# A cross-attention stage on one core: query copies laid once, stacks by one masked product, three PSUM banks in rotation

## What is computed

```python
q = _split_heads(query @ wq.T + bq, B)      # query: layernorm(x), 16 heads of depth 8
k = _split_heads(value @ wk.T + bk, B)      # value: context, 1500 rows
v = _split_heads(value @ wv.T + bv, B)
scores = jnp.einsum('bhqd,bhkd->bhqk', q, k) / scale
attn = jax.nn.softmax(scores, axis=-1)
ctx = jnp.einsum('bhqk,bhkd->bhqd', attn, v)
return ctx.transpose(0, 2, 1, 3).reshape(B, -1, D_MODEL) @ wo.T + bo
```

## Time and profile before

| | us |
|---|---|
| median of 3 runs | 771.29 (770.04 to 772.39) |
| the profiled execution | 769.12 |
| its span, first to last instruction | 767.3 |

### The profile page before, as it was taken

One profiled execution on the slowest core, in us unless ns is written; L12 is line 12 of the kernel. 1 busy time (PEld: TensorE's weight loads), 2 busy tenths in 40 slices (PEclk: granted clock), 3 DMA queues, 4 the chain that ended last, 5 costly groups with the idle time before them and its releaser, 6 DMA issues. The chain is left out here.

```text
span 767.3 us, 17218 instructions
## 1 busy us (share of the span) xinstructions
PE 665.7 (87%) x6570; PEld 520.1 (68%) x6570; DVE 465.4 (61%) x856; ACT 356.0 (46%) x533; POOL 200.1 (26%) x130
## 2 busy tenths in 40 slices
PE   1689968668999999999999999999999849999998
PEld 0334436435777777777777777777778738999997
DVE  4689737486665665675666666666577146443443
ACT  0335534413556556546555656555644625333321
POOL 2687323253123213213303312321300022111110
PEclk9999958867999999999999999999999958999999
DMA  5000000282165355435426426525526001111200
GB/s 192 0 1 1 1 0 1 49 175 61 51 153 122 86 116 120 104 96 124 120 77 155 109 61 155 120 63 137 121 50 156 3 9 43 43 41 43 80 14 25
DMA packets 16298, 59.04 MB, mean 77 GB/s; under 512 B 4488, under 2 KB 5384, under 8 KB 16264
## 3 DMA queue, kind: packets, MB, share of 16 engines
q1 hardware_dynamic: 16264, 58.57, 31.3%
HBM read 20.73 MB, written 0.46 MB: 28 GB/s over the span
## 5 line engine op out<-in xcount | busy, mean ns | idle before, releaser
L996 DVE TENSOR_REDUCE chunk_max<-PS 128x1 f32<-128x500 f32 x336 | 220.1, 671 | 114.2 <-PE PS L1093 113.6
L949 ACT ACTIVATE P<-PS 125x896 f32<-125x896 f32 x192 | 174.9, 918 | 137.5 <-PE PS L1123 132.2
L1093 PE MATMUL PS<-k_hi,q_block_hi 128*128 128x500 f32 x336 | 155.8, 483 | 11.8 <-DVE chunk_max L996 5.1
L1123 PE MATMUL PS<-q_stack,k_stack 97*125 97x224 f32 x768 | 123.0, 283 | 1.0 <-ACT P L949 0.8
L1123 PEld LDWEIGHTS PS<-q_stack,k_stack 97*125 97x125 f32 x768 | 108.4, 189 | 19.6 <-issue 10.9
L1093 PEld LDWEIGHTS PS<-k_hi,q_block_hi 128*128 128x128 f32 x336 | 65.5, 196 | 41.1 <-DVE chunk_max L996 24.5
L239 POOL TENSOR_TENSOR k_lo<-k_full,k_hi 128x500 fp32r<-128x500 f32 x48 | 60.1, 1254 | 102.4 <-ACT k_full L229 102.4
L1139 PE MATMUL PS<-P,values 125*32 125x112 f32 x3072 | 83.6, 260 | 0.0
L1139 PEld LDWEIGHTS PS<-P,values 125*32 125x32 f32 x3072 | 72.0, 110 | 15.0 <-issue 7.3
L1438 DVE TENSOR_TENSOR hidden<-gated,PS 128x448 f32<-128x448 f32 x64 | 39.5, 619 | 69.0 <-PE PS L1495 64.3
L913 POOL TENSOR_TENSOR q_block_hi<-q_hi,consts 128x896 fp32r<-128x896 f32 x16 | 27.4, 1715 | 192.7 <-PE PS L1109 188.4
(11 more groups left out here) (145 smaller groups left out, 824.9 us busy)
## 6 DMA issues: line engine op xcount, KB each, us to landing
k_stack<-k_hi SPq DMA_DIRECT2D x128, 187.5 KB, 4.7
ctxT<-ctx_in SPq DMA_DIRECT2D x16, 750.0 KB, 4.3
k_stack<-k_lo SPq DMA_DIRECT2D x64, 187.5 KB, 4.5
w_gate_up<-wgu_in SPq DMA_DIRECT2D x8, 512.0 KB, 4.0
w_down<-wd_in SPq DMA_DIRECT2D x8, 256.0 KB, 2.8
mats<-mats_in SPq DMA_DIRECT2D x1, 832.0 KB, 6.3
X<-x_in SPq DMA_DIRECT2D x1, 512.0 KB, 3.6
consts<-consts_in SPq DMA_DIRECT2D x1, 490.0 KB, 4.2
```

Of the source, the lines that this page charges most:

```text
L949: nc.scalar.activation(P[:, t % RING, :].rearrange("p (a n) -> p a n", a=2), PS[0:KR, 2 * (t % 2):2 * (t % 2) + 2, 0:HALF], ACT.Exp).then_ ...
L996: nc.vector.tensor_reduce(out=chunk_max[:, n // KC, n % KC:n % KC + 1], in_=PS[:, max_bank(b, j, n), 0:KW], axis=AX.X, op=ALU.max).then_in ...
L1093: nc.tensor.matmul(PS[:, max_bank(b, j, n), 0:KW], q_block_hi[:, j, 128 * t:128 * t + 128], k_hi[:, j, KW * c:KW * c + KW], start=True, st ...
L1123: last = nc.tensor.matmul(PS[0:KR, 2 * (t % 2) + g // 2, o:o + GH * N], k_stack[:, j, g, KR * t:KR * t + KR], q_stack[0:SHIFT_ROW + 1, j, ...
```

## The change

- **Query copies.** Before period 0 SyncE lays high, high and low parts of all queries, of each group of four heads, in `q_copies` on 96 partitions (`load_copies`, twelve DMAs, runs of 56 elements). `q_lo` as a tensor, `q_block_lo`, the selection matrices `sel` and `max_col` go.
- **Stack by one product.** GpSimd makes rows 0 to 95 of the whole stack by one multiplication of the batch's copies by the head mask (`stack_queries`).
- **Maxima by a transpose.** VectorE joins the maxima into `max_turn`, TensorE transposes them (`turn_max`, slots 3 and 8), ScalarE negates the 4 and 3 rows into `neg_rows`, and SyncE carries each row of 128 elements to row 96 of the stack by a DMA of its own (`load_shift`, 4 + 3 DMAs). Scores of slot 0 wait for them.
- **Three banks.** Chunks of the maximum, keys, values, output and turned maxima take banks 4, 5 and 7 in rotation (`bank_turns`: 30 uses in a period), each behind a wait for the reader of the use three before. The denominators move to the free half of bank 6, and the first weighing of a batch now waits for the reciprocals.
- **Keys.** ScalarE still reads each projection twice; the first read has a semaphore of its own, `k_hi_ready`, on which the chunks wait. Its waits for the free buffers stand behind the wait for the projection.
- **Order.** New `MAX_PLACES` (8 chunks ahead instead of 2) and new slots for all kinds. SyncE issues the stack first, then four rows, then the context, now of batch b+3, then three rows.

```diff
-            EARLY = 10
-            MAX_PLACES = [(1, 1, 0), (1, 1, 1), (1, 0, 0), (1, 1, 0), (1, 0, 0), (1, 1, 1),
-                          (1, 0, 0), (1, 1, 0), (1, 1, 0), (1, 1, 0), (0, 1, 0), (1, 0, 0)]
-            KEY_SLOTS, VALUE_SLOTS, STACK_SLOTS, DEN_SLOT, OUT_SLOT = [0, 1, 3], [2, 4, 5], [8, 10], 6, 11
-            RING, QUAD, WEIGH_SLOTS = 6, 4, [1, 5, 9]
+            EARLY = 8
+            MAX_PLACES = [(2, 0, 2), (0, 0, 0), (1, 2, 0), (1, 0, 0), (0, 1, 0), (1, 0, 1),
+                          (1, 0, 0), (1, 0, 0), (1, 0, 0), (2, 1, 1), (0, 0, 1), (0, 1, 1)]
+            KEY_SLOTS, VALUE_SLOTS, TURN_SLOTS = [2, 3, 4], [1, 6, 7], [3, 8]
+            SUMS_SLOT, DEN_SLOT, INVERT_SLOTS, SCALE_SLOT, OUT_SLOT = 1, 2, [3, 4], 4, 8
+            RING, QUAD, WEIGH_SLOTS = 6, 4, [0, 5, 9]
+            TURNING_BANKS = [4, 5, 7]
...
+            def bank_turns():
+
+                bank_of, uses = {}, 0
+                for t in range(KT):
+                    first, second, third = max_chunks(t)
+                    before = [("max", n) for n in first]
+                    for name, slots in (("key", KEY_SLOTS), ("value", VALUE_SLOTS), ("out", [OUT_SLOT]), ("turn", TURN_SLOTS)):
+                        if t in slots:
+                            before.append((name, slots.index(t)))
+                    for use in before + [("max", n) for n in (*second, *third)]:
+                        bank_of[use] = TURNING_BANKS[uses % len(TURNING_BANKS)]
+                        uses += 1
...
+                    def load_shift(b, j, a):
+
+                        sp.wait_ge(rows_ready, 2 * b + a + 1)
+                        for r, t in enumerate(range(HALF_TILES[a].start, HALF_TILES[a].stop)):
+                            sp.dma_start(q_stack[SHIFT_ROW:SHIFT_ROW + 1, j, 128 * t:128 * t + 128].bitcast(F32),
+                                         neg_rows[r:r + 1, j, a, :].bitcast(F32)).then_inc(shift_loaded[j], 16)
...
+                    load_copies()
+                    sp.wait_ge(v_projected, KC)
+                    load_ctx(sp, 2, 0)
+                    for a in range(2):
+                        load_shift(0, 0, a)
 
                     def period(b, j, u):
-                        if exists(b + 2, B):
-                            sp.wait_ge(cleared, 1)
-                            sp.wait_ge(v_projected, KC * (b + 1))
-                            load_ctx(sp, b + 2, j)
                         if exists(b + 1, B):
                             load_stack(b + 1, 1 - j)
+                            load_shift(b + 1, 1 - j, 0)
+                        if exists(b + 3, B):
+                            sp.wait_ge(v_projected, KC * (b + 2))
+                            load_ctx(sp, b + 3, 1 - j)
+                        if exists(b + 1, B):
+                            load_shift(b + 1, 1 - j, 1)
...
+                    def stack_queries(b, j):
+
+                        lay = [SHIFT_ROW, GROUPS, GH, N]
+                        own = C["quarter"][0:SHIFT_ROW, :].unsqueeze(1).unsqueeze(3).broadcast_to(lay)
+                        nc.gpsimd.tensor_tensor(
+                            q_stack[0:SHIFT_ROW, j, :].rearrange("p (g h n) -> p g h n", g=GROUPS, h=GH),
+                            q_copies[:, :, bass.ds(b, 1), :].bitcast(F32).broadcast_to(lay), own, ALU.mult
+                            ).then_inc(q_stacked, 1)
...
-                    def select_queries(b, j, a):
-
-                        pe.wait_ge(q_blocks, 2 * b + 2)
+                    def turn_max(b, a):
+
                         pe.wait_ge(max_ready, 2 * b + a + 1)
-                        shared_bank((q_stacked, 2 * b + a + 1))
...
+                        if later(b, 1):
+                            take_bank(BANK_OF["turn", a], (rows_ready, 2 * b + a + 1))
+                        elif a == 1:
+                            pe.wait_ge(rows_ready, 1)
+                        nc.tensor.transpose(turn_bank(b, a)[:, 0:128], max_turn[:, a, :], C["ident"]).then_inc(max_turned, 1)
 
                     def scores(b, j, u, t):
 
                         if t == 0:
                             pe.wait_ge(stack_loaded[j], 16 * STACK_DMAS * (u + 1))
-                            pe.wait_ge(q_stacked, 2 * (b + 1))
+                            pe.wait_ge(q_stacked, b + 1)
+                            pe.wait_ge(shift_loaded[j], 16 * QT7 * (u + 1))
```

More of the change, by code:

```diff
@@ L216, in first_keys, with read_keys @@
                 project_keys(pe, b, b, 0, c)
[L218 to L223, removed]
+        def read_keys(act, b, j, u, c, bank=MISC):
             if later(b, 1):
@@ L227, in read_keys, with split_keys @@
             k = slice(KW * c, KW * c + KW)
[L228 to L232, removed]
+            if c == 0 and later(b, 2):
+                act.wait_ge(stack_loaded[j], 16 * STACK_DMAS * u)
+                act.wait_ge(max_scored, QT7 * KC * (b - 1))
+            nc.scalar.activation(k_hi[:, j, k], bank[:, 0:KW], ACT.Identity, bias=COL["bk"]).then_inc(k_hi_ready, 1)
+            nc.scalar.activation(k_full[:, k], bank[:, 0:KW], ACT.Identity, bias=COL["bk"]).then_inc(k_ready, 1)
+        def split_keys(pool, b, j, u):
             if later(b, 2):
@@ L824, in max_batch, with bank, max_bank, turn_bank @@
                 return (b + 2, j) if t >= EARLY else (b + 1, 1 - j)
-            STACK_DMAS = 3 * GROUPS
+            def bank_turns():
[9 more added lines that the diff above has]
+                        uses += 1
+                assert uses % len(TURNING_BANKS) == 0
+                return bank_of
+            BANK_OF = bank_turns()
+            def bank(name, n):
+                return PS[:, BANK_OF[name, n], :]
+            def max_bank(b, n):
+                return BANK_OF["max", n] if later(b, 1) else (n + 4) % 6
+            def turn_bank(b, a):
+                return bank("turn", a) if later(b, 1) else MISC
             q_all = sb2("q_all", [128, B * PITCH])
@@ L865, in build @@
             OSUM = PS[:, 6, 0:4 * N]
+            DEN = PS[:, 6, 4 * N:8 * N]
+            OUT2 = bank("out", 0)[:, 0:D]
             with nc.Block() as block:
@@ L1017, in invert @@
                         dve.wait_ge(den_done, b + 1)
-                        nc.vector.reciprocal(heads_out2[:, half], MISC[:, half]).then_inc(den_inverted, 1)
+                        nc.vector.reciprocal(heads_out2[:, half], DEN[:, half]).then_inc(den_inverted, 1)
                     def scale_heads(b):
@@ L1147, in denominators @@
                         pe.wait_ge(o_copied, b + 1)
[L1148 to L1149 removed]
+                        nc.tensor.matmul(DEN, C["den"], heads_sum[:, :], start=True, stop=True
                                          ).then_inc(den_done, 1)
```

174 lines of the change are left out of this document (89 added, 85 removed).

## The result

The changed kernel takes 714.79 us (median of four runs, 713.22 to 717.7), beside 770.66 us for the kernel before on the same chip: a ratio of 0.929 [0.924, 0.934]. The forecast was 708.0 us with a range of 698 to 730, so the median is 6.8 us above it and inside the range. The profiled execution took 713.22 us, span 711.4; before it was 769.12 and 767.3.

A forecast was written before the change was run, and what follows sets the result against it. TensorE was taken to bound the kernel. Gains of -1.4 (start), 4.1 (first period), 55.5 (thirteen steady periods) and 5.1 (last but one) sum to 63.3 us, taking the median 771.29 to 708.0; range 698 to 730.

The forecast's parts named there:

- Work per period: TensorE, steady period: 24.21 us of work, less 1.82 for the selections, plus 0.54 for two transposes, gives 22.93.
- both turnings: TensorE, two transposes of the maxima per period: 0.27 us each, 0.54 together, from eight like them taking 2.16.
- a changed pitch of the weighings: Sign of a wrong prediction: TensorE's start-to-start time for a block of weighings differs from 1.97 us.
- Waits of the rotation: Three banks: slot 3's chunk waits about 0.6 us for the keys' bank, slot 0's scores 0.1; period 23.6.
- Thirteen periods: Steady periods 1 to 13 of the cross attention: each falls from 27.87 to 23.6 us, 55.5 gained.
- Row DMAs: Last three shift rows before slot 0's scores: a 5.1 us chain just hidden by 5.1 us of TensorE work.
- Rival A: Scores of slot 0: late row DMAs set the period, 24.4 us (time 718) to 25.8 (736); chance 0.27.
- Period 14: Last period but one, 13 chunks and no keys: 18.65 us plus 0.7, so 19.4, a gain of 5.1.
- Rival B: TensorE's waits only move to other places, ScalarE's key reads above all; only the selection gains, 751 us; chance 0.06.
- Rival C: Slower than before: shift rows wait behind larger transfers at slot 0; break-even 4.9 us a period; chance 0.04.
- Before period 0: Start of batch 0's scores, after query copies, GpSimd's product and row DMAs: net 1.4 us later.
- Period 0 and period 15: First period 21.7 us, a gain of 4.1, with 1.5 for the low clock; last period unchanged, gain 0.

The follow-up runs named there:

- The kernel without the key wait: Changed kernel, but ScalarE reads each key projection from PSUM once and makes the rounded copy from SBUF: 707.92 us.
- the rows cut in two: Changed kernel with each row of shifts carried by two DMAs of 64 elements instead of one of 128: 726.97 us.
- The kernel with 3.6 us of it: Changed kernel with the old chunk places (two ahead instead of eight), maxima turned at slots 8 and 10: 817.98 us.
- the filled kernel: Changed kernel with chunks two ahead, plus 15 short unused matmuls ahead of the scores of slot 0: 782.61 us.

## Why the prediction was right, and where it was off

**Work per period (22.93): the sum fits, two of its terms do not.** The kernel without the key wait has a period of 22.90 to 22.97. Luck has a part in that. The changed kernel in order of time:

```profile
291.61 1.00 PE L196 MATMUL PS<-ctxT,mats 128*128 128x500 f32 x2
...
292.99 1.01 PE L196 MATMUL PS<-ctxT,mats 128*128 128x500 f32 x2
...
294.71 0.39 PE L1155 MATMUL PS<-k_hi,q_block_hi 128*128 128x500 f32 x1
295.03 1.74 PE L1195 MATMUL PS<-P,values 125*32 125x112 f32 x64
296.70 0.49 PE L1155 MATMUL PS<-k_hi,q_block_hi 128*128 128x500 f32 x1
297.03 0.60 PE L1179 MATMUL PS<-q_stack,k_stack 97*125 97x224 f32 x4
```

From 291.61 to 292.99 stand a key projection, a turning and the scores of a slot: 1.38 us, less 0.84 and 0.44 leaves 0.10 for the turning. The second one, between output projection and scores, makes their 1.55 us 1.61. So both turnings cost 0.16 us and not 0.54. That price was taken from the duration of eight transposes in a row, not from what one adds between other work. From 294.71 to 297.03 stand two chunks and a block: 2.32 us, so the block takes 1.88 and not 1.97; the distance of 2.41 in the earlier trace rows held a little wait. With these two terms the work is about 22.3. The other 0.6 us of the 22.9 are delays of 0.1 to 0.2 that the forecast had at nothing or in its 0.7: a chunk next to keys or to the output projection takes 0.33 and not 0.22, and slot 0's scores come 0.2 late. The forecast had named a changed pitch of the weighings as a sign of being wrong, and by that sign this term was off by 5%. Reading distances from start to start was still the better way: before's busy time was 25.93 where its work by this sum is at most 24.21.

**Waits of the rotation (0.7 above 22.93): right in place, high by 0.2.** The chunk of slot 3 waits for ScalarE's second read as walked, 0.4 us and not 0.6, and slot 0's scores come 0.2 late and not 0.1; the period is 23.44 and not 23.6. That these waits were worth removing, and that the shared bank had held them, the kernel without the rotation shows by 4.7 us a period. Thirteen periods: 57.7 gained, 55.5 forecast.

**Row DMAs ("just hidden", 5.1 against 5.1): the term of the chain was mis-sized.** Issue 0.59 and not 0.79, landing 2.1 and not 2.7; the rows overlap as forecast, the chain is 3.9 us and leaves 1.2 free, as the rows cut in two confirm. Rival A had its chance of 0.27 from a slack of nil that is not there. It came true in one period only, the last:

```profile
538.88 0.67 PE L1179 MATMUL PS<-q_stack,k_stack 97*125 97x224 f32 x4 [1.20 <-DMA q_stack<-neg_rows]
```

Period 14 has no keys to project and fewer chunks, so TensorE has 3.5 us of work behind the turning (534.18) instead of 5.1, and the chain took 4.7 there (to 538.88). The forecast took the steady waits over to a period with less cover: 20.96 and not 19.4.

**Rival B: refuted.** The period stands 0.5 us above the sum of work, not 3.7, and ScalarE's second read accounts for 0.54.

**Rival C: not met, and its price was wrong.** It priced a wait at its own length and put the break-even at 4.9 us a period. The kernel with 3.6 us of it is already 6.5% slower than before, with 0.9 us of other waits in its period. A period of 27.9 would have been near the kernel before, as the filled kernel is with 1.6% above it; the fallen clock makes the rest.

**Before period 0 (-1.4): -2.25, and another mechanism.** The forecast followed the copies, GpSimd's product and the row DMAs. What stands last ahead of the first scores is TensorE's own work:

```profile
184.86 0.78 PE L1155 MATMUL PS<-k_hi,q_block_hi 128*128 128x500 f32 x1 [0.36 <-ACT neg_rows L1002]
186.51 4.07 PE L1155 MATMUL PS<-k_hi,q_block_hi 128*128 128x500 f32 x7 [0.86 <-DVE chunk_max L1056]
190.37 1.01 PE L1179 MATMUL PS<-q_stack,k_stack 97*125 97x224 f32 x4
```

Eight chunks stand behind the last turning (184.03), where before there were two; they and a wait for VectorE take 5.5 us, at a granted clock of 0.50 from 184 us on, the 1.2 GHz level. That they are scored ahead was named in the forecast as a fact and given no price. They cost less than these 5.5 us: the last row is issued by 186.6 and with a landing of 2.1 would be there at about 188.7 (an estimate), so without them the scores would start some 1.7 us sooner. The 4.7 us ahead of this stretch are of the two executions compared: a collision that the other profiles don't have, and a place that moves by 8 us between executions without one.

**Period 0 and period 15.** Period 0 took 22.84 against 21.7: the granted clock was 0.91, against 0.94 in the longer stretch of before; by the lost share, 0.09 x 22.84 - 0.06 x 25.82, that is an estimate of 0.5 us of the 1.1, and the rest was not traced. Period 15 was taken as unchanged and took 1.5 us more. Two rows of it, in order of time:

```profile
543.09 0.65 PE L1204 MATMUL PS<-heads_sum,consts 128*128 128x224 f32 x2 [0.81 <-ACT heads_sum L1014]
...
559.41 1.80 PE L1211 MATMUL PS<-mats,heads_out 128*56 128x128 f32 x8 [2.09 <-DVE heads_out L1082]
```

The denominators, now at slot 2, wait 0.8 us for ScalarE's copy of the sums; in the kernel before, in its later slot, they had no such wait in this period. The same wait of 0.8 stands there in the kernel run again. And the last output projection takes 1.80 us where the kernel before took 1.08 for the same eight, behind the same wait: a lower clock, which did not come again (1.08). The changed kernel's interval from the last copy of sums but one to the last was 13.58 in this execution and 15.15 when it was run again, so such ends move by 1.5 us between executions of one kernel; in the slower one a block of weighings behind a short wait takes 2.83 us instead of 1.74.

**Sum.** In the profiled executions 55.9 us gained (769.12 to 713.22) against 63.3. The miss of 7.4 (7.6 in the stretches of the table) is 4.7 of the late start, 0.9 of the stretch before period 0, 1.1 of period 0, 1.6 of period 14 and 1.5 of period 15, less 2.2 that the steady periods gave more. The kernel run again took 712.03, its profiled execution, without the late start, 710.31. The median of 714.79 is 6.8 above the forecast of 708, and only the profiled execution can be divided so; what the other three lost is not known.

## What to carry to other kernels

Add up the work of the bounding engine from start-to-start distances and walk its order once with every reader of every buffer: that gave the steady period within 1%, here with some luck, since terms too high by 0.6 us stood for delays that were left out. Price an instruction by what it adds between its neighbours, not by its duration. The other misses were at the ends, where fewer instructions cover the same chains and TensorE's clock is low. When a step runs further ahead, price that work at the front as well. A wait of several microseconds on TensorE in each turn of a loop must be priced with the clock that falls behind it, here nearly twice its length.

## What the runs showed of the hardware that was not expected

- One VectorE operation of 0.34 us took 6.5 us, in one execution, beside a GpSimd key difference of 1.24 us and the fill of 5.22 us behind it.
- The scaling of the heads (L1082) takes 1.48 us where it took 0.38 before. It now starts with a key difference of GpSimd and ends 0.25 us behind it:

```profile
294.00 1.48 DVE L1082 TENSOR_TENSOR heads_out<-heads_out,heads_sum 128x224 f32<-128x224 f32 x1
```

```profile
293.97 1.26 POOL L234 TENSOR_TENSOR k_lo<-k_full,k_hi 128x500 fp32r<-128x500 f32 x1 [1.42 <-ACT k_full L225]
```

  These 1.1 us are all of the rise of VectorE's busy time in a period, 18.01 to 18.95; in the last batch, which has no key difference beside it, the same operation takes 0.39 us. It costs nothing, since nobody waits for it here. The page "SBUF — State Buffer" of the Trainium skill says the same of a VectorE operation with two inputs from SBUF beside a GpSimd operation that reads it.
- Idle waits of 3.55 to 3.73 us on TensorE in periods of 30.7 went with a granted clock of 0.89; the same waits filled with useless matmuls went with 1.00.
- An fp32 matmul of 64 columns with its weight load, repeated, takes 0.23 us, as much as a chunk of 500 columns, whose operands are fp32r, with its own (0.22).
